# Dealing the value, rest and projection products of two attention layers out over the gaps between score tiles

## The reference, cut to what matters

```python
q = (xn @ w_q).reshape(B, SQ, NUM_HEADS, DIM_HEAD)
kv = context @ w_kv
k, v = jnp.split(kv, 2, axis=-1)
...
scores = jnp.einsum('bqhd,bkhd->bhqk', q * SCALE, k)
attn = jax.nn.softmax(scores, axis=-1)
out = jnp.einsum('bhqk,bkhd->bqhd', attn, v).reshape(B, SQ, INNER)
out = out @ w_out + b_out
```

## Time and profile before

| | before |
|---|---|
| three runs | 1208.56, 1210.32, 1219.51 us; median 1210.32 |
| the profiled execution | 1213.6 us, its span 1211.9 us |
| busy share of the span | PE 85%, weight loads 65%, DVE 60%, ACT 52%, POOL 47% |
| mean granted clock of TensorE | 0.922 of full speed |
| steps of layer 2 / layer 3 | from 526.7 us / from 866.3 us of the span, 16 each |

### The profile page before, as it was taken

How to read it: one execution, slowest core, us unless ns; L and a number is a source line. 1 busy time by engine, 2 the same in 40 slices (tenths; PEclk the granted TensorE clock), 3 DMA queues, 4 the chain that set the end, 5 groups by cost and what they waited for, 6 DMA issues and landing times.

```text
span 1211.9 us, 21865 instructions
## 1 busy us (share of the span) xinstructions
PE 1035.8 (85%) x6575; PEld 782.6 (65%) x6575; DVE 724.8 (60%) x2474; ACT 627.3 (52%) x2087; POOL 572.2 (47%) x926
## 2 busy tenths in 40 slices
PE   4988899869889988979999997676789999987995
PEld 3875788835556667856667665566566676654994
DVE  5565264476776772387877775322877777852444
ACT  2344323347778714358777763223387777731221
POOL 5223665452000142657555656366375556665552
PEclk9987999978999989979999997788889999987997
DMA  3003556599700124023223311354342223214676
GB/s 64 13 27 98 174 165 208 168 157 358 267 2 1 35 63 142 35 88 118 75 88 105 115 45 44 89 177 133 88 122 89 88 71 105 71 34 129 203 208 174
DMA packets 157284, 134.30 MB, mean 111 GB/s; under 512 B 20907, under 2 KB 131171, under 8 KB 157168
## 3 DMA queue, kind: packets, MB, share of 16 engines
q1 hardware_dynamic: 146560, 114.18, 31.8%
q0 software_dynamic: 8448, 17.20, 4.3%
q10 hardware_dynamic: 2160, 1.53, 0.5%
HBM read 80.77 MB, written 52.08 MB: 110 GB/s over the span
## 4 chain that ended last, share of the span: by engine, by line
PE 62%; DVE 15%; issue 7%; ACT 6%; DMA 3%; POOL 3%; another core or an unknown queue 2%; SPq 1%; ACTq 0%; DVEq 0%; POOLq 0%
PE ps L2829 5%; PE ps L2921 4%; PE ps L3043 4%; PE ps L2934 4%; PE ps L2831 4%; PE ps L2830 4%; PE ps L3025 3%; PE ps L3571 3%; PE ps L3575 3%; PE ps L3224 2%; ACT ex L1365 2%; PE ps L3057 2%; PE ps L3584 2%; DVE ln_st L1770 2%
## 5 line engine op out<-in xcount | busy, mean ns | idle before, releaser
L1365 ACT ACTIVATE ex<-ps,nmx 128x154 f32<-128x154 f32 x512 | 194.3, 391 | 83.7 <-DVE nmx L2320 82.3
L1127 POOL TENSOR_TENSOR pp<-ex,rc 128x256 f32<-128x256 f32 x256 | 157.6, 616 | 143.7 <-DVE rc L2325 143.0
L2320 DVE TENSOR_REDUCE nmx<-ps 128x2 f32<-128x308 f32 x256 | 118.1, 463 | 49.9 <-PE ps L2831 48.9
L2829 PE MATMUL ps<-kp,q_s 128*128 128x308 f32 x256 | 99.5, 389 | 25.2 <-ACT ex L1365 22.8
L964 POOL DMA_INDIRECT yq_d<-yq,ids_q x78 | 74.7, 957 | 78.2 <-DVE yq L2072 58.7
L1365 ACT ACTIVATION_READ_ACCUMULATOR ex<-ps,nmx 128x1 f32 x512 | 104.7, 205 | 0.0
L1482 ACT ACTIVATE pe<-ps,nmx 128x154 f32<-128x154 f32 x256 | 84.9, 394 | 31.9 <-DVE nmx L2203 30.8
L2829 PEld LDWEIGHTS ps<-kp,q_s 128*128 128x128 f32 x256 | 51.1, 200 | 57.5 <-ACT ex L1365 30.9
L934 POOL TENSOR_TENSOR ln_r<-ln_v,mhalf 128x4 f32<-128x4 f32 x32 | 32.7, 1021 | 103.5 <-DVE ln_v L1778 86.1
L2830 PE MATMUL ps<-kp,q_s 128*128 128x308 f32 x256 | 81.5, 318 | 0.0
L2831 PE MATMUL ps<-kp,q_s 128*128 128x308 f32 x256 | 81.2, 317 | 0.0
(11 more groups left out here) (484 smaller groups left out, 2861.2 us busy)
## 6 DMA issues: line engine op xcount, KB each, us to landing
w_r<-in_L_ffn_W SPq DMA_DIRECT2D x69, 256.0 KB
xq_d<-blankq SPq DMA_DIRECT2D x4, 4160.0 KB, 23.8
pt_d<-pt_b SPq DMA_DIRECT2D x60, 256.0 KB, 2.1
pt_pair<-pt_d SPq DMA_DIRECT2D x120, 128.0 KB, 2.8
w_q<-in_L_ffn_W SPq DMA_DIRECT2D x46, 256.0 KB
w_q<-in_L_ffn_w SPq DMA_DIRECT2D x46, 128.0 KB
xq<-xq_d SPq DMA_DIRECT2D x24, 130.0 KB
w_s<-in_L_ffn_W SPq DMA_DIRECT2D x8, 256.0 KB
```

Source lines behind the costliest of these rows:

```text
L1127: pool.tensor_tensor(pp[st % 2][:, m % 4, 2 * j:2 * j + 2, :], w[:, :, 0:P], r.broadcast_to([P, 2, P]), ALU.mult)
L1365: ins = act.activation(ex[:, tt % NEX, j, :], ps[:, tt % 3, j * SK:(j + 1) * SK], ACT.Exp, bias=nmx8[:, tt % 8, j:j + 1], accum_out=sm8[:, ...
L2320: dve.tensor_reduce(nmx8[:, tt % 8, :], ps[:, tt % 3, 0:2 * SK].rearrange("p (h s) -> p h s", h=2), AX.X, ALU.max, negate=True).then_inc(n ...
L2829: mm(bank, w[0], x[0], start=first, stop=False)
```

## The change

Four things are altered, with no instruction added or taken away.

1. In the PE loop of a step, `rest_values` moves from the end of the step to the gap after s0 of the next step (so it is two steps late in the loop: `st - 2`), v0 to the gap after s5, `project` to the gap after s6; v1 stays after s7. The preparation items move to other gaps: p0 and p1 one score tile later, p2 to after T3, p3 to after T4. T2 moves one tile earlier, and T4 to the gap after s4.
2. The ACT and DVE loops and the list of names follow that order: both `high_out` copies of a step now stand after the exponentials of tiles 1 and 2, before the preparation items' copies.
3. In item 12 (line 2987) the loop over heads now runs inside the loop over batches.
4. The same exchange of loops stands in the small value products of attention 2 (line 3185).

```diff
@@ ring
-            names += turned(st - 1, 1) * late + spot(0) + spot(1) + behind("A") + [("pt", st - 1, 2)] * late
-            names += [("pt", st - 1, 3)] * late + [("y", st - 2)] * later + [("pt", st - 1, 4)] * late + spot(2) + behind("C")
-            names += spot(3) + behind("D") + turned(st, 0)
+            names += spot(0) + [("pt", st - 1, 2)] * late + spot(1) + behind("A") + [("pt", st - 1, 3)] * late + spot(2) + behind("C")
+            names += [("pt", st - 1, 4)] * late + spot(3) + [("y", st - 2)] * later + behind("D") + turned(st, 0)
@@ heads, ACT
                     exps(st, 0)
+                    exps(st, 1)
+                    high_out(st - 2, 0)
+                    step_prep(st, 0)
+                    exps(st, 2)
                     high_out(st - 2, 1)
-                    step_prep(st, 0)
-                    exps(st, 1)
+                    copy_pt(st - 1, 2)
                     step_prep(st, 1)
...
-                    exps(st, 2)
-                    copy_pt(st - 1, 2)
                     exps(st, 3)
+                    step_prep(st, 2)
...
                     exps(st, 4)
                     exps(st, 5)
                     copy_pt(st - 1, 4)
-                    step_prep(st, 2)
...
+                    step_prep(st, 3)
                     exps(st, 6)
...
-                    step_prep(st, 3)
                     exps(st, 7)
-                    high_out(st - 1, 0)
+                    if st == NST - 1:
+                        high_out(st - 1, 0)
@@ heads, DVE
                     maxima(st, 0)
-                    low_out(st - 2, 0)
-                    copy_pt(st - 1, 1)
...
                     maxima(st, 2)
-                    low_out(st - 2, 1)
+                    low_out(st - 2, 0)
                     step_prep(st, 1)
...
                     maxima(st, 3)
-                    copy_pt(st - 1, 3)
+                    low_out(st - 2, 1)
...
                     maxima(st, 4)
+                    copy_pt(st - 1, 3)
+                    step_prep(st, 2)
...
                     maxima(st, 5)
-                    add_up(st - 2)
+                    step_prep(st, 3)
...
                     turn_blocks(st, 1)
-                    step_prep(st, 2)
...
                     maxima(st, 7)
-                    step_prep(st, 3)
+                    add_up(st - 2)
@@ prep, PE (item 12)
-                    for h in range(4):
-                        for b in range(B):
+                    for b in range(B):
+                        for h in range(4):
@@ heads, PE
                     scores(st, 0)
-                    transposes(st - 1, 1)
+                    rest_values(st - 2)
+                    scores(st, 1)
                     step_prep(st, 0)
-                    scores(st, 1)
+                    transposes(st - 1, 2)
+                    scores(st, 2)
                     step_prep(st, 1)
...
-                    scores(st, 2)
-                    transposes(st - 1, 2)
                     scores(st, 3)
                     transposes(st - 1, 3)
-                    scores(st, 4)
-                    scores(st, 5)
-                    project(st - 2)
-                    transposes(st - 1, 4)
                     step_prep(st, 2)
...
+                    scores(st, 4)
+                    transposes(st - 1, 4)
+                    step_prep(st, 3)
+                    scores(st, 5)
+                    values(st - 1, 0)
                     scores(st, 6)
-                    step_prep(st, 3)
+                    project(st - 2)
                     scores(st, 7)
-                    values(st - 1, 0)
                     values(st - 1, 1)
-                    rest_values(st - 1)
+                    if st == NST - 1:
+                        rest_values(st - 1)
```

More of the change, by code:

```diff
@@ L1412, in heads @@
                         turned_x(3)
-                    exps(st, 2)
-                    copy_pt(st - 1, 2)
                     exps(st, 3)
+                    step_prep(st, 2)
+                    if st == 0:
+                        turned_x(2)
                     exps(st, 4)
@@ L1418, in heads @@
                     copy_pt(st - 1, 4)
-                    step_prep(st, 2)
-                    if st == 0:
-                        turned_x(2)
+                    step_prep(st, 3)
                     exps(st, 6)
```

## The result

The changed kernel took **1269.31 us** (median of four runs, 1265.39 to 1275.06), the kernel before 1212.12 in the same comparison: ratio **1.047, interval 1.040 to 1.053**, slower. 1255 was forecast, with 1234 to 1277 as the range. The profiled execution took 1275.06 us, its span 1273.3, mean granted clock 0.911 (before 0.922).

A forecast was written before the change was run, and what follows sets the result against it. PE was taken to set most steps, losing time mostly waiting for exponentials. From 1213.6 us profiled, +38.2 for steps 4 to 11, -1 loops and +8 clock gave 1258.8; less 3.3 to the median, 1255 us, range 1234 to 1277.

The forecast's parts named there:

- The mechanism: In steps 4 to 11, ACT's late key copies hold up DVE, then maxima and exponentials: +38.2 us for both layers.
- heavy step: Any of steps 4 to 11 of a layer, with preparation items; forecast at 15.7, 14.7, 12.8 or 15.7 us by kind.
- Steps 4 and 8: Steps where preparation item 0 lengthens the first round trip through ACT and DVE: 15.7 us against 14.57, +1.1 each.
- path to p3: In steps 4 and 8, from score tile 1's last matmul until PE starts the last preparation place: 8.3 us.
- The clock: PE's idle time in steps 4 to 11 lowers its granted clock: 0 to 24.8 us possible, 8 taken.
- five falls: Number of clock falls taken for the sixteen steps 4 to 11 of both layers: 8 us together, 1.55 us per fall.
- the rival with falls in every heavy step: Clock falls in each of steps 4 to 11, in some twice: 1273 to 1290 us, chance 0.10.
- The separated products: PE's three small-product runs, now apart, cost 1.21 us each: 0.55 more a step, 8.8 in sixteen steps.
- Light steps and edges: Steps 2, 3, 12, 13: -0.7 to +2.2 us each; steps 0, 1, 14, 15: -6 to +13 for eight; both taken 0.
- The loops: Exchanged loops in item 12 and attention 2's small products: 0 to -9.6 us outside PE's waits, taken -1.
- the full 24.8 of the clock: Upper end for the clock: one fall in each of the sixteen steps 4 to 11 of both layers, 24.8 us.
- The rivals that the gaps fill or even out: Between score tiles: waits vanish, about 1187 us, chance 0.06; or even exchange, 1203 up to 1218 us, chance 0.08.

## Why the prediction was right, and by how much it was off

- **The mechanism stood, and its size too.** At full clock the four kinds of heavy step last 15.77, 14.93, 12.85 and 16.29 (the last from the run with PE kept busy) against 15.7, 14.7, 12.8 and 15.7. For both layers, with layer 3's sum taken for layer 2 as well, that is 2 x 119.7 - 2 x 98.7 = 42 us; the forecast said 38.2. The links were tested singly: the low parts, T3's bank, both, all copies, and ACT's late copies in the old order of PE.
- **Steps 4 and 8** were the coarsest: +1.7 in place of +1.1. The path to p3 was right: in the run with PE kept busy, step 8 starts p3 (item 2, line 2976) 1006.86 - 998.56 = 8.30 behind the last matmul of s1, where the forecast had 8.3, and there too T3's copy is what it waits for. What was mis-sized lies behind p3: item 2 and s5 take 1008.12 - 1006.86 = 1.26, where the sum had two pieces of 0.42, so 0.42 of the 0.6 that the step lasts longer than forecast. PE's two waits of 2.0 us for item 0's last copy in layer 2 lie ahead of p3 and add nothing to this path; they matter to the clock.

```profile
998.56 0.30 PE L2831 MATMUL ps<-kp,q_s 128*128 128x308 f32 x1
...
1006.86 1.13 PE L2976 MATMUL ps<-w_raw,ctxT 128*128 128x256 f32 x4 [0.83 <-DVE pt_s L2334]
...
1008.12 0.30 PE L2831 MATMUL ps<-kp,q_s 128*128 128x308 f32 x1
```

- **The clock was mis-sized.** The sum took five falls, 8 us. The heavy steps' 260.2 less 2 x 119.7 at full clock is 20.8. Before, they held 2.3 over four times the full-clock steps (199.7 less 197.4), of which 1.55 is the fall in step 8 of layer 3 and 0.8 a longer step 6 of layer 2 at full clock (12.72). So the clock added some 18 to 19. Both factors were low. Nine heavy steps fell, eight of them to 0.81 or 0.82; and a fall cost some 2.2 us (step 10 pays 18.36 - 15.77 = 2.6), not 1.55. In us the rival with falls in every heavy step was nearer than the forecast. The five had no row behind them, and the waits of a step would not have given one: before, steps 4 and 8 of both layers had the same three waits of PE (0.25 to 0.27, 0.72, 0.97 to 0.98), and three of the four ran at 1.00, one at 0.89. What decides it stays open here. That the clock has a share at all, the run with PE kept busy shows.
- **The separated products** were priced rightly, and they are part of the 42 us. All three runs stand behind p3, on the chain: v0 takes 1061.11 - 1059.62 = 1.49, less two ordinary starts 1.21, v1 1.22 and the rest 1.21 in the same way, where the forecast had 1.21 each. So the 0.55 a step that it took for two separations (8.8 in the sixteen heavy steps) is paid in full; one alone measured 0.35 in the kernel before.

```profile
1059.62 0.31 PE L2831 MATMUL ps<-kp,q_s 128*128 128x308 f32 x1
1059.86 1.08 PE L3043 MATMUL ps<-pt_pair,vv 128*64 128x512 f32 x4
...
1061.11 0.31 PE L2830 MATMUL ps<-kp,q_s 128*128 128x308 f32 x1
```

- **Light steps and edges**: taken 0; steps 2, 3, 12 and 13 gave +4.7 over both layers, steps 0, 1, 14 and 15 -1.4. v0 did wait for its DMA now, as feared, but 1.2 us in all.
- **The loops**: taken -1; by themselves -2.4 (-6 to +1).
- Sum: 42 + 18.5 + 3.3, less 2.5 outside the two layers' steps, is 61, the growth of the span. The profiled execution was the longest of four; by the median it was 57, of which the forecast had 45. Most of what it lacked is the clock, and the range held it only because its upper end had the full 24.8 of the clock in it.

The rivals that the gaps fill or even out failed as argued: PE's wait for exponentials before score tiles did fall by 14 us, and the round trips took more.

## What to carry to other kernels

When the order on one engine moves, write down for each copy which engine's result it waits for and what stands behind it. Here a copy by one engine, its second half by another and a maximum behind that closed a loop that cost its full length (1.92 us later, 1.91 us longer), and no PE work later in the step made it up. Count such a loop before counting the gap that the change fills. Then ask what the new waits do to the clock, and don't judge that by one step: here steps with the same waits ran at either level.

## What the runs showed of the hardware

- The same waits of PE left the clock up in one step and brought it down in another: after the change, step 10 had waits of 0.70, 1.52 and 1.34 us in layer 3 at 1.00 and the same in layer 2 at 0.81. Before, the last of three waits in layer 3's step 4 (at 1.00 throughout) and step 8 (0.89):

```profile
919.34 0.41 PE L2829 MATMUL ps<-kp,q_s 128*128 128x308 f32 x1 [0.97 <-ACT ex L1365]
968.64 0.50 PE L2829 MATMUL ps<-kp,q_s 128*128 128x308 f32 x1 [0.98 <-ACT ex L1365]
```

- In step 4 of layer 3 after the change, the clock fell behind a single wait; PE's row with the wait in brackets, and the granted clock of the stretches ahead of it and behind it:

```profile
955.02 0.45 PE L2829 MATMUL ps<-wqT,wkT 128*128 128x128 f32 x1 [1.99 <-DVE wkT L1886]
```

```profile
950.00:955.00 5.00, 3.03 (x25) 2.63 (x22) 1.82 (x6) 2.84 (x12) 1.77 (x6) 1.00 0.41 109
955.00:961.80 6.80, 6.40 (x24) 5.63 (x25) 4.02 (x10) 3.90 (x15) 2.53 (x6) 0.50 0.00 0
```

  The clock is at 1.00 up to the end of the wait of 1.99 and at 0.50, which is 1.2 GHz, right behind it, while PE is busy again. So the price is paid in the busy part that follows, not in the wait.
- Sixty-four products a layer of no use, put into PE's waits in the heavy steps, made the kernel some 13 us shorter.
- Between two score tiles a run of small products cost 0.35 us more than next to other small products (12.06 against 11.69); those of item 12 took half as long with the column groups in turn (0.65 against 1.39).
